# Each output projection of the first token tile in two pieces of six matmuls, in the last head of the attention

## The reference

```
q1, q2, k1, k2 = heads of x @ Wq1, Wq2, Wk1, Wk2          # 16 heads of 16
v = heads of x @ Wv                                       # 16 heads of 32
a1 = softmax(causal(q1 k1^T / 4)); a2 = softmax(causal(q2 k2^T / 4))
out = (a1 - lam[head] * a2) @ v
normed = (out - mean(out)) * rsqrt(var(out) + 1e-5)       # over the 32 values of a head
x = layernorm(x + (normed * (1 - LAM_INIT)).merged @ Wo)
h = silu(x @ w1) * (x @ w2); h = gelu(h @ h1); h = gelu(h @ h2)
x = layernorm(x + h @ w3)
```

## Time and profile before

| | before |
|---|---|
| median of 3 runs | 1904.69 us (1902.13 to 1904.76) |
| the profiled execution: its own time | 1904.57 us |
| its span, first to last instruction | 1902.8 us |
| mean granted TensorE clock | 0.992 |
| TensorE matmul (PE) busy | 1854.8 us, 97% |
| ScalarE (ACT) busy | 1408.3 us, 74% |
| VectorE (DVE) busy | 1029.9 us, 54% |
| GpSimd (POOL) busy | 233.2 us, 12% |

### The profile page before, as it was taken

One profiled execution on the slowest core, in us unless ns is written; L12 is line 12 of the kernel. 1 busy time (PEld: TensorE's weight loads), 2 busy tenths in 40 slices (PEclk: granted clock), 3 DMA queues, 4 the chain that ended last, 5 costly groups with the idle time before them and its releaser, 6 DMA issues.

```text
span 1902.8 us, 30777 instructions
## 1 busy us (share of the span) xinstructions
PE 1854.8 (97%) x12160; PEld 1062.0 (56%) x12160; DVE 1029.9 (54%) x1999; ACT 1408.3 (74%) x1701; POOL 233.2 (12%) x308
## 2 busy tenths in 40 slices
PE   8997999999999999999999999999999999999996
PEld 6773333333333333333333335888888888888885
DVE  5554665566456655655566565454545454636342
ACT  4546999999999999999999997444545454545352
POOL 3001112111111112111211121000000000000000
PEclk9997999999999999999999999999999999999998
DMA  8877066335643664456535621000010101000000
GB/s 274 253 255 162 7 117 122 65 70 112 122 73 69 110 117 78 75 100 117 91 69 92 117 60 43 25 12 34 12 34 12 34 12 34 15 31 23 1 12 13
DMA packets 130176, 146.09 MB, mean 77 GB/s; under 512 B 74260, under 2 KB 100500, under 8 KB 122388
## 3 DMA queue, kind: packets, MB, share of 16 engines
q1 hardware_dynamic: 129304, 142.46, 34.6%
q10 hardware_dynamic: 720, 1.57, 0.2%
HBM read 101.79 MB, written 39.06 MB: 74 GB/s over the span
## 4 chain that ended last, share of the span: by engine, by line
PE 86%; DVE 4%; issue 1%; DVEq 0%; ACT 0%; PEldq 0%
PE attn_sums_ps L987 26%; PE split_hid_ps L1586 25%; PE attn_s_ps L964 20%; PE split_hid_ps L1570 6%; PE split_y_ps L1603 3%; PE split_y_ps L1527 2%; PE attn_sums_ps L995 2%; PE split_turn_ps L1515 1%; DVE attn_raw L1127 1%; DVE attn_raw L1116 1%; DVE attn_sums_sb L1111 0%; DVE attn_diff L1132 0%; DVE ffn_r L1091 0%; PE attn_sums_ps L1017 0%; DVE attn_total L1134 0%
## 5 line engine op out<-in xcount | busy, mean ns | idle before, releaser
L937 ACT ACTIVATE attn_probs<-attn_s_ps 128x1024 f32<-128x1024 f32 x1088 | 1002.8, 1127 | 21.8 <-PE attn_s_ps L964 21.3
L987 PE MATMUL attn_sums_ps<-attn_probs,heads_v 128*32 128x512 f32 (+3 forms) x5120 | 588.7, 541 | 0.0
L964 PE MATMUL attn_s_ps<-heads_q,heads_k 50*128 50x512 f32 (+3 forms) x2560 | 451.6, 427 | 12.7 <-DVE heads_q L1069 12.3
L964 PEld LDWEIGHTS attn_s_ps<-heads_q,heads_k 50*128 50x128 f32 x2560 | 213.2, 185 | 448.0 <-ACT attn_probs L937 401.4
L1671 ACT ACTIVATE split_whole<-split_hid_ps,scales 128x512 f32<-128x512 f32 x128 | 88.3, 690 | 273.9 <-PE split_hid_ps L1586 273.7
L917 POOL TENSOR_SCALAR_AFFINE_SELECT attn_probs<-attn_probs 128x512 f32<-128x512 f32 x256 | 180.6, 717 | 842.9 <-ACT attn_probs L937 842.9
L1586 PE MATMUL split_hid_ps<-split_hid_b,ffn_r 128*128 128x512 f32 x1024 | 240.8, 392 | 0.0
L1586 PE MATMUL split_hid_ps<-split_hid_a,ffn_r 128*128 128x512 f32 x1024 | 238.0, 391 | 0.0
L1586 PEld LDWEIGHTS split_hid_ps<-split_hid_a,ffn_r 128*128 128x128 f32 x1024 | 190.2, 188 | 41.0 <-DVE split_hid_a L1811 0.5
L1586 PEld LDWEIGHTS split_hid_ps<-split_hid_b,ffn_r 128*128 128x128 f32 x1024 | 189.8, 188 | 38.2
L987 PEld LDWEIGHTS attn_sums_ps<-attn_probs,heads_v 128*32 128x32 f32 x5120 | 107.8, 108 | 175.8 <-issue 141.7
(11 more groups left out here) (163 smaller groups left out, 1665.7 us busy)
## 6 DMA issues: line engine op xcount, KB each, us to landing
heads_q_raw<-qk_raw SPq DMA_DIRECT2D x60, 384.0 KB
heads_k_raw<-qk_raw SPq DMA_DIRECT2D x60, 384.0 KB
qk_raw<-proj_copies SPq DMA_DIRECT2D x64, 256.0 KB, 2.7
values<-proj_v SPq DMA_DIRECT2D x8, 1024.0 KB, 6.1
heads_k_raw<-ones SPq DMA_DIRECT2D x60, 128.0 KB
heads_v<-values SPq DMA_DIRECT2D x15, 512.0 KB, 19.1
heads_spare<-in_ffn SPq DMA_DIRECT2D x30, 256.0 KB, 9.5
diffs<-attn_diff SPq DMA_DIRECT2D x30, 256.0 KB, 4.1
```

What stands on the lines that cost most here:

```text
L937: nc.scalar.activation(weights, side_by_side, ACT.Exp, scale=SCALE).then_inc(exp_done, 1)
L964: last = nc.tensor.matmul(s_ps[(NU * h + n) % SLOTS][:, s, col:col + width], k_sb[u][rows, b * SEQ + j * PARTS:b * SEQ + (j + 1) * PARTS], ...
L987: last = nc.tensor.matmul(sums[c * D:(c + 1) * D, off:TILE], v_sb[u][:, b * KEY_BLOCKS + j, :], probs[k % PROBS][:, b, s, place:place + wi ...
```

## The change

`project(s)` gets a second argument, the chunks it is to do. Chunks 0 and 1 (six matmuls) become the piece `begin`, chunks 2 and 3 (six matmuls) the piece `end`; only the last signals VectorE. The table `EARLY` places them behind two successive weighings:

| piece | weighing before | weighings after |
|---|---|---|
| project(0) | 16 | 15 and 16 |
| turn_heads(1) | 17 | 17 |
| project(1) | 19 | 19 and 20 |
| turn_heads(2) | 23 | 23 |
| project(2) | 25 | 25 and 26 |
| turn_heads(3) | 26 | 27 |
| project(3) | 28 | 29 and 30 |
| turn_mid(0), turn_mid(1) | 32 | 32 |

The core of the diff (in the changed kernel the lines below the table are 2 higher, those below `project` 11 higher):

```diff
-        EARLY = {END[1] + 4: [("turn", 0)], END[1] + 7: [("project", 0)], END[1] + 8: [("turn", 1)], END[1] + 10: [("project", 1)],
-                 END[2] + 3: [("turn", 2)], END[2] + 5: [("project", 2)], END[2] + 6: [("turn", 3)], END[2] + 8: [("project", 3)],
+        EARLY = {END[1] + 4: [("turn", 0)], END[1] + 6: [("begin", 0)], END[1] + 7: [("end", 0)], END[1] + 8: [("turn", 1)],
+                 END[1] + 10: [("begin", 1)], END[1] + 11: [("end", 1)],
+                 END[2] + 3: [("turn", 2)], END[2] + 5: [("begin", 2)], END[2] + 6: [("end", 2)], END[2] + 7: [("turn", 3)],
+                 END[2] + 9: [("begin", 3)], END[2] + 10: [("end", 3)],
                  END[2] + 12: [("mid", 0), ("mid", 1)]}
...
-            def project(s):
+            def project(s, chunks):
...
                 pe.wait_ge(early_low, s + 1)
-                for c in range(VC):
+                for c in chunks:
...
-                last.then_inc(early_projected, 1)
+                if VC - 1 in chunks:
+                    last.then_inc(early_projected, 1)
```

More of the change, by code:

```diff
@@ L1018, in project, with begin_project, end_project @@
                                                 start=(c == 0 and i == 0), stop=(c == VC - 1 and i == len(EARLY_PASSES) - 1))
-                last.then_inc(early_projected, 1)
+                if VC - 1 in chunks:
+                    last.then_inc(early_projected, 1)
+            def begin_project(s):
+                project(s, range(VC // 2))
+            def end_project(s):
+                project(s, range(VC // 2, VC))
             def turn_mid(c):
@@ L1044, in use @@
                     for what, n in EARLY.get(k, []):
-                        {"turn": turn_heads, "project": project, "mid": turn_mid}[what](n)
+                        {"turn": turn_heads, "begin": begin_project, "end": end_project, "mid": turn_mid}[what](n)
             def head(h, u, r, first, last):
```

## The result

| | before | changed |
|---|---|---|
| runs beside each other | 1903.34 us median of 6 (1902.13 to 1904.76) | 1909.85 us median of 6 (1907.77 to 1911.03) |
| ratio, 95% interval | | 1.0034 [1.0022, 1.0045] |
| ratio of a second measurement | | 1.0028 [1.0016, 1.0040] |
| the profiled execution, its span | 1904.57 us, 1902.8 us | 1908.11 us, 1906.4 us |
| PE, ACT, DVE, POOL busy | 1854.8, 1408.3, 1029.9, 233.2 us | 1854.1, 1409.0, 1030.3, 235.9 us |

The changed kernel is slower by 0.3%, at the forecast 1909.3 us within the spread of its runs.

A forecast was written before the change was run, and what follows sets the result against it. The prediction took TensorE to be saturated from 1137 to 1174 us, with the chain then passing over VectorE's layernorm to turn_mid. Its terms, 3.09 + 0.84 + 0.80 = 4.73 us, gave 1904.57 + 4.73 = 1909.3 us, range 1906.8 to 1911.5.

The forecast's parts named there:

- Term 1: Projection 3 ends two pairs of scores and weighings later, so VectorE's layernorm behind it starts 3.09 us later.
- Term 2: First half of projection 0, behind weighing 15, waits on TensorE for VectorE's split of row 0: 0.84 us.
- Term 3: Four cuts ahead of projection 3's end each add a block's beginning and end, 0.20 us: 0.80 us in all.
- The sum: The three terms added, 3.09 + 0.84 + 0.80 = 4.73 us, moving turn_mid's start from 1174.16 to 1178.89.
- The clock: Rival: TensorE's clock falls to half in the new 3.24 us gap at turn_mid, +7 us, 1916.3 us; chance 0.07.
- ScalarE: Rival: ScalarE sets the pace from 1137 to 1174 us; halves remove its gaps, 1903.4 us, not slower; chance 0.05.
- The cover of weighing 21: Weighing 21 needs rows 0 and 1 added; the add still fits by 0.13 us less 0.04, so no cost.
- The shift passes on whole: Behind turn_mid, the splits and the finish's start follow from it, so the full delay reaches the finish.

The follow-up runs named there:

- e1: Kernel before with only projection 3 moved, whole, from behind weighing 28 to behind 30; ratio of runs to before 1.0013 [1.0004, 1.0022].
- e2: Kernel before with only projection 0 cut in halves, behind weighings 15 and 16; finish starts 1.15 us later, ratio to before 1.0002 [0.9993, 1.0011].
- e3: Kernel before with projections 1, 2 and 3 cut, first halves one weighing ahead so ends stay put; projection 0 whole; ratio to before 0.9999 [0.9990, 1.0008].
- e6: Changed kernel with projection 0 whole again behind weighing 16; finish at 78.46 us from the last head's first scores, ratio to before 1.0016 [1.0007, 1.0025].
- e7: Kernel before, projections whole: projection 2 one weighing earlier, projection 3 two, turn of row 3 and turn_mid's first half one; ratio to before 0.9991 [0.9982, 1.0000].

## Why the prediction was right

The forecast was +4.73 us. From the last head's first scores to the finish it is 5.47 and 5.54 us in two executions. The three terms account for 4.8 us of that, and the clock, which the sum left out, for the rest.

- **Term 1**, two pairs less behind projection 3: forecast 3.09, measured 3.07 (e1). The wait of `turn_mid` that follows was forecast as 3.24 us and is 3.28.
- **Term 2**, the early half's stall: forecast 0.84, measured 0.94 (e2). The place of the half was right; the time from VectorE's end to TensorE's start was 0.13 us (1136.43 to 1136.56 in the trace after), not 0.04.
- **Term 3**, a block's ends: forecast 0.20 for each cut, measured 0.18 (e3). The Trainium skill's figures by columns alone ("TensorE: Matmul & The Clock Gate", "Back-to-back issue gap") leave this cost out. They are near to the pitch inside a block, 0.119 us, but a cut is not free here.
- **The sum** holds to the start of `turn_mid`: 74.75 and 74.62 against 69.82, 4.93 and 4.80 us. Counted from the turn of row 0 it is 45.87 and 45.86 us against 41.06: 4.8 us in both.
- **The clock** is the step that failed. I gave the fall in the gap a chance of 0.07 and a price of 7 us. It fell in all four profiled executions with this gap (the changed kernel twice, e1, e6), in none of the seven without, and costs 0.55 to 0.80 us: `turn_mid` to the finish takes 4.73 to 4.98 us instead of 4.18. It does not fall at the same place each time: in the trace after the first transposes already ran at 0.50, in e1 the clock was still 1.00 from 1176.8 to 1177.8 us, behind the start of `turn_mid` at 1176.83, and 0.50 from 1178 us on. Two inferences were wrong. That a mean of 0.95 over 150 to 155 us means that 3 us of idle time are harmless took one fall as a limit for others. And the length of the low stretch was taken over from the attention's start, where it was still 0.50 at 175 us, nearly 14 us behind the start of TensorE's work; here it was full again 3.1 to 4.5 us behind the start of `turn_mid`. The prediction also did not see that 0.80 us of idle time ahead of the finish stood ready to take a part of any such cost. The Trainium skill's rule on idle gaps ("TensorE: Matmul & The Clock Gate", "Why this matters for your kernels") was the better guide, and the trace agrees, with 0.50 behind 3.28 us of idle time.
- **Luck.** The event that I held for unlikely came about, and at the price that I gave it the time would have been 1916.3 us, far outside the stated range. That the measured 1909.85 us lies inside is owed to a cost under 1 us that I had not worked out.
- **ScalarE** does not set the pace (e3). Its gaps behind six of the eight halves are 0.34 to 0.62 us, a quarter to six tenths of those at the same places before, near the third to a half that was forecast; behind the half that waited and behind the last one they are 1.47 and 1.30 us, which was not forecast. There are eleven gaps instead of seven, and the sum did not fall: 37.00 - 30.43 = 6.57 us idle in the window from 1137 to 1174 us of after, against 5.81 in that of before (the work in the two is not quite the same). As long as TensorE sets the pace, ScalarE's idle time is only dealt out anew.
- **The cover of weighing 21** held: no wait stands there.
- **The shift passes on whole** into the finish, which takes 724.0 to 724.7 us in all eleven traces.

The medians differ by 6.5 us in one measurement and the ratio of the other gives about 5.3; 5.5 lies within both intervals. More than that the runs do not resolve.

## What to carry to other kernels

Where an engine is full, as TensorE is here, cutting its work finer does not help the engine that waits for it (e3). Look instead at what stands ahead of the last piece on which another engine's long chain depends, and move that piece to the earliest place at which its operands are ready (e7). Before a piece is moved ahead, compare the end of its producer with the new place to a tenth of a us; here 0.9 us too early was paid in full. Count a gap of TensorE like the one of 3.28 us here as more than itself: the work behind it ran at half clock in four of four profiles. And look for idle time further down the path before pricing a slowdown: of the 1.4 us that the low clock added to TensorE's work in the trace after, 0.80 fell where TensorE had been idle.

## What the runs showed of the hardware

Two stretches ahead of the last head spread from execution to execution, whatever the kernel: the time to the first scores of the first head, 160.8 to 163.2 us in the eleven traces, and the first head itself, 63.3 to 65.4 us. For the second the traces show a reason. Behind the idle stretch at the attention's start the clock stays at 0.50 for a time that differs from execution to execution. In the window from 170.5 to 175 us it was still 0.50 in the trace of before and already 1.00 in the trace after, in lines of the windows of the two:

```profile
170.50:175.00 4.50, 4.50 (x32) 1.74 (x32) 0.69 (x1) 2.71 (x4) 0.64 (x1) 0.50 1.01 168
```

```profile
170.50:175.00 4.50, 4.50 (x48) 1.69 (x44) 0.69 (x1) 4.31 (x6) 0.64 (x1) 1.00 1.04 166
```

The first head takes 65.2 to 65.4 us in the five executions of the first sort and 63.3 to 63.8 us in the six of the second; kernels with halves and kernels with whole projections are found in both sorts. The next fourteen heads take 877.6 to 877.7 us in all. So a change of 1 us behind them is read from a fixed point inside the trace, not from the run's time.
